# Turning probabilities and queries as rounded halves (float32r) instead of float32, in an attention and mixture-of-experts layer on one core

## What is computed

```python
def attention(x, ctx, mask, wq, wk, wv, wo):        # B, L, D = 8, 512, 512; H, KVH, DK = 16, 2, 32
    Q = rope((layernorm(x) @ wq) by heads)           # [B, 16, 512, 32]
    K = rope((ctx @ wk) by heads), V = ctx @ wv      # 2 heads, each used by 8 query heads
    scores = einsum('bhqd,bhkd->bhqk', Q, K) / sqrt(DK)
    attn = softmax(where(mask == 0, -1e9, scores), axis=-1)
    out = einsum('bhqk,bhkd->bhqd', attn, V)
    return out by tokens @ wo
x = x + attention(layernorm(x), ctx, ...)
x = x + experts(layernorm(x)) + shared(layernorm(x))
```

## Time and profile before

| | |
|---|---|
| time, median of 3 runs | 1426.14 us (1424.04 to 1426.2) |
| span of the profiled execution (first to last instruction) | 1422.9 us |
| TensorE, matmuls: busy | 1373.1 us, 97% |
| TensorE, weight loads: busy | 1067.2 us, 75% |
| VectorE: busy | 960.4 us, 67% |
| ScalarE: busy | 844.9 us, 59% |
| GpSimd: busy | 581.4 us, 41% |
| granted TensorE clock, mean | 0.994 |

### The profile page before, as it was taken

How to read it: one execution, slowest core, us unless ns; L and a number is a source line. 1 busy time by engine, 2 the same in 40 slices (tenths; PEclk the granted TensorE clock), 3 DMA queues, 4 the chain that set the end, 5 groups by cost and what they waited for, 6 DMA issues and landing times.

```text
span 1422.9 us, 28293 instructions
## 1 busy us (share of the span) xinstructions
PE 1373.1 (97%) x8110; PEld 1067.2 (75%) x8110; DVE 960.4 (67%) x2655; ACT 844.9 (59%) x1951; POOL 581.4 (41%) x724
## 2 busy tenths in 40 slices
PE   6898999999999999999898999999999999999997
PEld 4675777877777777777576777777777888888885
DVE  6888888888888888988777666666653334333342
ACT  2788979889798897988983222222213434444342
POOL 4443523435244343342253432333334555555553
PEclk9899999999999999999999999999999999999999
DMA  5545464564645646445465222222257779785542
GB/s 203 152 145 146 135 190 139 152 185 137 188 136 149 187 131 190 142 140 157 114 202 203 85 87 90 82 75 84 73 140 205 201 178 260 204 197 103 111 76 37
DMA packets 146070, 206.62 MB, mean 145 GB/s; under 512 B 35456, under 2 KB 73088, under 8 KB 145923
## 3 DMA queue, kind: packets, MB, share of 16 engines
q1 hardware_dynamic: 124562, 166.91, 38.1%
q0 software_dynamic: 17952, 33.64, 12.3%
q10 hardware_dynamic: 3408, 4.26, 0.9%
HBM read 105.49 MB, written 69.35 MB: 123 GB/s over the span
## 4 chain that ended last, share of the span: by engine, by line
PE 82%; DVE 6%; ACT 4%; issue 3%; DMA 2%; SPq 1%; POOL 1%; DVEq 0%; POOLq 0%; ACTq 0%
PE psum L693 13%; PE psum L1494 13%; PE psum L1496 12%; PE psum L1495 12%; PE psum L808 7%; PE psum L787 7%; PE psum L738 3%; PE psum L739 3%; PE psum L740 3%; ACT a_probs L591 2%; PE psum L1561 2%; PE psum L708 2%; DVE a_probs L955 1%; ACT a_probsT L597 1%; PE psum L1590 1%
## 5 line engine op out<-in xcount | busy, mean ns | idle before, releaser
L591 ACT ACTIVATE a_probs<-a_probs,a_low 128x512 f32<-128x512 f32 x512 | 366.6, 716 | 83.7 <-DVE a_low L955 82.2
L955 DVE CUSTOM_DVE_ANT_0 a_probs<-psum,a_bias 128x512 f32<-128x512 f32 x512 | 345.4, 685 | 76.5 <-PE psum L787 73.2
L693 PE MATMUL psum<-a_ident,a_probs 128*128 128x128 f32 x2048 | 311.0, 274 | 7.8 <-ACT a_probsT L597 5.9
L693 PEld LDWEIGHTS psum<-a_ident,a_probs 128*128 128x128 f32 x2048 | 245.3, 141 | 77.0 <-issue 25.6
L787 PE MATMUL psum<-a_kT,a_q_stack 128*128 128x512 f32 x512 | 247.2, 484 | 10.1 <-DVE a_low L955 5.4
L597 ACT ACTIVATE a_probsT<-psum 128x512 f32<-128x512 f32 x328 | 190.7, 582 | 10.0 <-PE psum L693 10.0
L1363 POOL DMA_INDIRECT out<-b_y,b_pairs_sb x71 | 112.6, 1586 | 148.7 <-DMA out<-b_y,b_pairs_sb 85.9
L1795 DVE SCALAR_TENSOR_TENSOR b_v_hidden<-b_v_hidden,psum 128x256 f32<-128x256 f32 x71 | 29.9, 421 | 165.9 <-ACT b_v_hidden L1459 165.9
L961 DVE COPY a_probsT<-psum 128x512 f32<-128x512 f32 x184 | 126.0, 685 | 6.1 <-PE psum L693 4.2
L1494 PE MATMUL psum<-b_w,b_vT_hi 128*128 x284 | 117.4, 413 | 0.1
L808 PE MATMUL psum<-a_probsT,a_v 128*32 128x512 f32 x1024 | 116.7, 595 | 0.0
(11 more groups left out here) (218 smaller groups left out, 3054.3 us busy)
## 6 DMA issues: line engine op xcount, KB each, us to landing
b_w<-w_halves SPq DMA_DIRECT2D x16, 1536.0 KB
a_q_stack<-a_qT_hi SPq DMA_DIRECT2D x254, 64.0 KB, 2.0
a_q_stack<-a_qT_lo SPq DMA_DIRECT2D x253, 64.0 KB, 2.0
w_halves<-a_w_hi SPq DMA_DIRECT2D x96, 128.0 KB, 2.0
w_halves<-a_w_lo SPq DMA_DIRECT2D x96, 128.0 KB, 1.9
a_xT_in<-in_x_turned SPq DMA_DIRECT2D x32, 256.0 KB, 2.9
a_ctx_in<-in_ctx SPq DMA_DIRECT2D x32, 256.0 KB, 3.0
a_x_in<-in_x SPq DMA_DIRECT2D x32, 256.0 KB, 3.2
```

Of the source, the lines that this page charges most:

```text
L591: nc.scalar.activation(probs[:, h % 2, t], probs[:, h % 2, t], ACT.Exp, bias=low[:, h % H, t:t + 1], scale=-1.0, accum_out=total[:, h // G ...
L693: last = nc.tensor.transpose(out[:, P * i:P * (i + 1)], src(i), identity[:])
L955: nc.vector.tensor_tensor_reduce(probs[:, h % 2, t], psum[:, t % 2], bias[:, t], 1.0, HUGE, ALU.add, ALU.min, low[:, h % H, t:t + 1]).then ...
```

## The change

Two more tiles are laid over bytes that are there already: `probs_bits` over `probs` and `q_bits` over `q`, of the same shapes and of type float32r. The helper `four` reads them, takes `ident_r` in place of `ident`, and its result in PSUM is declared as float32r. So the 2048 transposes of probabilities and the 128 of queries are asked for in float32r. Their sources are not rounded ahead, the writers and the evacuations keep their types, and the transposes of the feed-forward phase stay as they were.

```diff
+    def bits(name, shape):
+
+        return nc.alloc_sbuf_tensor_at(f"a_{name}_bits", shape, F32R, offset=base + ATTENTION_PLACES[name])
+
...
+    probs_bits = bits("probs", [P, 2, TT, L])
+    q_bits = bits("q", [P, 2, TT, D])
...
-        def four(out, src, identity):
+        def four(out, src):
             for i in range(4):
-                last = nc.tensor.transpose(out[:, P * i:P * (i + 1)], src(i), identity[:])
+                last = nc.tensor.transpose(out[:, P * i:P * (i + 1)].bitcast(F32R), src(i), ident_r[:])
             return last
...
-            four(in_ring(part, b, "qT", i), lambda t: q[:, batch, t, P * g:P * (g + 1)], ident).then_inc(s["qT_filled"], 1)
+            four(in_ring(part, b, "qT", i), lambda t: q_bits[:, batch, t, P * g:P * (g + 1)]).then_inc(s["qT_filled"], 1)
...
-            four(out, lambda c: probs[:, h % 2, t, P * c:P * (c + 1)], ident).then_inc(s["t_filled"], 1)
+            four(out, lambda c: probs_bits[:, h % 2, t, P * c:P * (c + 1)]).then_inc(s["t_filled"], 1)
```

## The result

| | before | after |
|---|---|---|
| time, median | 1425.21 us (6 runs, 1424.04 to 1426.2) | 1416.17 us (6 runs, 1411.92 to 1422.6) |
| span of the profiled execution | 1422.9 us | 1413.1 us |
| granted TensorE clock, mean of it | 0.994 | 0.986 |

The ratio is 0.9937, with a 95% interval of 0.9917 to 0.9957: 9 us faster, or 0.6%. The forecast was 42 us less, so the sign was right and the size was not, and 1416 lies outside the range of 1360 to 1408. The title's "rounded halves" names a type: these turnings read the old bytes as float32r, and nothing is split into halves for them.

The account below looks back on a forecast made before the run. PE was taken to bound the kernel; six middle bodies giving 34 us, the first 5, the last 2.5 and the start 0.4, about 42 in all, brought 1426.1 to 1384 us. The 8-in-10 range was 1360 to 1408.

Parts of the forecast that it names:

- What bounds the kernel: Middle attention bodies: PE has no slack, busy 88.76 of 89.20 us; DVE (77.38) and ACT (77.20) follow it.
- What a turning costs before: Float32 turnings at L693: they start 0.109 us apart, and that distance is what PE pays.
- What a turning costs after: Float32r turnings at L693: 0.060 us apart, taken from L715 and L728, so each saves 0.049 us.
- The windows of 5.6 us: Half a middle body in four-unit windows, each as long as its busiest engine: 41.96 of 44.8 us, 5.6 saved per body.
- the ends: Gains outside the six middle bodies: first body 5 us, last body 2.5, query turnings of the start 0.4.
- what is costed at nothing: New tiles, writers, evacuations, float32r into PSUM, POOL, DMA share (0.54 to 0.58) and feed-forward phase: no cost expected.
- Rival 1: Attention bodies: two score banks limit the slack, only 2.8 us saved per body, 21 in all, 1405 us; chance 0.19.
- Rival 2: Attention bodies: engines even out nearly fully, down to DVE's 77.4 us, 79 us saved, 1347 us; chance 0.07.
- Rival 3: Turnings: loads bound them, or float32r of unrounded numbers runs as before; no change, 1426 us; chance 0.04.
- Rival 4: Attention bodies: a less busy PE gets half-clock dips of 13.6 us, each losing about 5.7; slower, 1435 us; chance 0.04.

Follow-up runs that it names:

- three_of_four: Changed kernel without the fourth turning of every unit and of every turned query tile: 1417.35 us (8 runs), 0.9932 of the kernel before.
- probe: Changed kernel plus five runs of 16 identity turnings at the start, float32r with loads of 128, 64, 32, 128 columns and float32 with 128: 1419.02 us (one run).
- two_of_four: Changed kernel with only the first two turnings of every four made: 1421.68 us (8 runs), 0.9966 of the kernel before.

## Why the prediction was wrong, step by step

- **What bounds the kernel** was right for the kernel before: PE was busy 88.76 of 89.20 us and its lines made up 93% of that body's chain. It stopped being right after a gain of 2.2 us: three_of_four takes 4.3 us more from PE and a quiet body stays at 85.9 to 87.1.
- **What a turning costs before**, 0.109, was right: 0.108 to 0.110 in the probe.
- **What a turning costs after, 0.060, is the step that failed.** In a run it is 85 to 87 ns, so that 0.024 is saved there, half of the 0.049. Of the two witnesses, L728 has a load of only 8 columns, and the probe shows narrow loads to be free (60 ns from turning to turning at 64 and 32). The other was a pair. Its loads in the trace of before:

```profile
346.86 0.35 PEld L715 LDWEIGHTS psum<-a_ident_r,a_k_stack 128*128 128x128 f32 x2
```

  The first load began at 346.86, 0.21 us ahead of the first turning at 347.07, under the scores before it. The second began with the first turning, and then there was no third. I read from "the second turning comes 0.06 later" that a load fits into 0.06. The pair says nothing of that: the distance that counts is from a load to the next behind it. In a unit of four one load runs ahead, so the first two distances are still 62 and 66 ns, and then the loads, some 85 apart, set the pace: 85 ns to the fourth turning and 87 to the scores, whose own load stands in the same row. Before, the slower float32 turnings left room for that load, and the scores followed after 28 ns. The prediction had no term for the scores' load. Together it is 0.0165 saved for each turning, not 0.049: 36 us of PE time in all instead of 107.
- **The windows of 5.6 us** come out at the true size, worked out afterwards. With 0.0165 in place of 0.049 they give 5.60 + 5.60 + 3 x 5.40 + 5.56 + 5.60 + 5.25 = 43.8 of 44.8, so 2.0 us in a body; measured 2.2 in a quiet one and 1.6 as the mean of six. With the ends cut in the same ratio (a third of 7.9) the sum would be 6 x 2.0 + 2.6 = 14.6, and the time 1411.5. One agreement at a small size doesn't prove the method, as the next step shows.
- **At the size of the forecast they would not have held**, and this is the second step that failed. Already with three_of_four they ask for 85, and the quiet bodies are 85.9 to 87.1. two_of_four brings PE to 77.4 us in a body, near the 75.4 that the forecast had, and its quiet bodies are 85.6 to 86.6, where I expected 83.6 at PE 75.4. What the windows left out is, for a part, the transfers: "what is costed at nothing" looked at GpSimd and at the DMA share of 0.54, and not at the 63 us of issuing on SyncE behind it. With fewer copies the body is 84.2.
- **Rival 1** had 86.4 for a body. Its number fits two_of_four, but it named the two score banks as the reason, and the table above shows the copies with ACT and DVE behind them. No run changed the number of score banks. **Rival 2** had no part in it.
- **Rival 3** was closer than I gave it, for the loads do set the pace. But its rule gives 107 ns for 128 columns (the Trainium skill, TensorE: Matmul & The Clock Gate, section LDWEIGHTS; the formula there has no term for the type), and the probe shows 81 to 89 from turning to turning. By that rule nothing would have been gained; the trace disagrees. That float32r of unrounded numbers would run as before is refuted by the rows of the turning above.
- **Rival 4**, the clock, came in part, beside a gain instead of in its place: 21 us more at half clock. By estimate it cost about 2 in the first body, up to 1.7 in the third middle one and 1.4 behind attention, where nothing was changed. It expected dips of 13.6 us in the bodies; there they are of 3.4. By the sentence from the Trainium skill (same page, PE-mode transpose) that turnings don't count, the prediction took it that less turning would change nothing. The trace disagrees: the change and three_of_four, which differ from before in turnings alone but for a few at the start, had 39.3 and 74.2 us at half clock for 17.9. So either turnings keep the clock up or the time that PE stands brings it down; these runs don't part the two.

From 1411.5 to the measured 1416.2 are 4.7 us. In the profiled execution the clock and the two waits for the keys make up about as much. That split is an estimate from single stretches, and no run shows it.

## What to carry to other kernels

The cost of an instruction in a run is read from three or more of the same form with the same load; a pair or a first one is served by what ran ahead. Count also what stands behind the run: here the scores, held up by their load, took back half of what the turnings had saved among themselves (59 of 114 ns in a unit). When a bound engine is eased, list the transfers and the issue time of the DMA queues beside the engines; here relief of any single one of the four brought 1.4 us or less in a quiet body, and of all four 7. And look at the granted clock afterwards in stretches that the edit didn't touch: a less busy TensorE was paid back there in part.

## What the runs showed of the hardware that I had not expected

- In a run, a float32r turning of 128 x 128 starts every 85 to 87 ns, set by its load of 128 columns; with 64 or 32 columns every 60, set by itself. In float32 it is 108 to 111 (probe).
- One load runs ahead of a run: the first two of four wide turnings still follow after 62 and 66 ns, and the product behind the run starts 87 ns after it instead of 28 (before and after).
- A mean clock lower by 0.007 between two runs of one and the same kernel went with 10.7 us in 1413.
- A block of `weighted` in two halves takes 2 x 1.87 us of PE and in one piece 3.57. The single records (379 and 592 ns) would make the difference look far larger than it is.
- An issue of a copy took 0.59 us on SyncE (L379) and that of a weight load 0.45 us on SyncE and 0.56 us on GpSimd.
